# A language-model tower on one core: the first sequence's embedding rules applied by masked matmuls in place of a sort

## The reference

```python
def _L0_tok_ref(token_ids, base_embeddings, rule_transform, token_rules):
    base_embeds = base_embeddings[token_ids]
    rule_indices = token_rules[token_ids]
    rule_matrices = rule_transform[rule_indices]
    return jnp.einsum('bsd,bsde->bse', base_embeds, rule_matrices)

h = _L0_tok_ref(x, base_embeddings, rule_transform, token_rules)
h = h + _L0_attn_ref(_layernorm(h), Q, K, VO)
h = h + _L0_ffn_ref(_layernorm(h), Wg, bg, bias, W1, b1, W2, b2)
```

## Time and profile before

| | us |
|---|---|
| median of 3 runs | 624.54 |
| lowest, highest | 620.55, 628.31 |
| the profiled execution, by its own time | 619.58 |
| its span from first to last instruction | 617.5 |
| PE busy in the span | 499.3 (81%) |
| DVE busy | 410.7 (67%) |
| ACT busy | 287.2 (47%) |
| POOL busy | 228.3 (37%) |

### The profile page before, as it was taken

How to read it: one execution, slowest core, us unless ns; L and a number is a source line. 1 busy time by engine, 2 the same in 40 slices (tenths; PEclk the granted TensorE clock), 3 DMA queues, 4 the chain that set the end, 5 groups by cost and what they waited for, 6 DMA issues and landing times.

```text
span 617.5 us, 9436 instructions
## 1 busy us (share of the span) xinstructions
PE 499.3 (81%) x2732; PEld 268.7 (44%) x2732; DVE 410.7 (67%) x1003; ACT 287.2 (47%) x581; POOL 228.3 (37%) x375
## 2 busy tenths in 40 slices
PE   0066603778679896999999999999999989999985
PEld 0035501234444342445544544454454444575753
DVE  5532486645215874978869877895975776665577
ACT  0203301025545543456564565556456546547664
POOL 5664356463225300340254145122413313181542
PEclk9998755559979997999999999999999999999989
DMA  8815212733381062440440422044042200000000
GB/s 234 312 59 152 79 36 61 179 95 103 95 229 40 14 155 53 102 113 5 100 114 2 102 63 60 1 104 113 1 96 68 53 2 2 11 2 10 11 2 17
DMA packets 21791, 47.05 MB, mean 76 GB/s; under 512 B 6248, under 2 KB 11576, under 8 KB 21680
## 3 DMA queue, kind: packets, MB, share of 16 engines
q1 hardware_dynamic: 15408, 32.23, 21.5%
q0 software_dynamic: 4752, 8.20, 4.9%
q10 hardware_dynamic: 1584, 6.03, 3.0%
HBM read 9.97 MB, written 11.01 MB: 34 GB/s over the span
## 4 chain that ended last, share of the span: by engine, by line
PE 54%; DVE 19%; issue 8%; DMA 6%; POOL 6%; ACT 3%; SPq 3%; another core or an unknown queue 0%; DVEq 0%; ACTq 0%; POOLq 0%
PE bank L1274 14%; PE bank L1260 10%; PE bank L1240 7%; PE bank L1202 4%; PE bank L1224 4%; DVE mx L997 3%; POOL emb_sorted L527 2%; DMA ctxT<-in_table,ids 2%; PE bank L1196 2%; PE bank L1197 2%; DVE r_sb L1055 2%; POOL ctxT L517 2%; PE bank L1132 2%; POOL r_sb L591 2%; DMA ks<-qk_l 1%
## 5 line engine op out<-in xcount | busy, mean ns | idle before, releaser
L997 DVE TENSOR_REDUCE mx<-bank 128x1 f32<-128x512 f32 x256 | 170.5, 687 | 83.5 <-PE bank L1260 75.3
L591 POOL TENSOR_TENSOR r_sb<-r_sb 128x256 f32<-128x256 f32 x174 | 91.0, 523 | 251.8 <-DVE r_sb L1073 171.4
L671 ACT ACTIVATE prob<-bank 128x512 f32<-128x512 f32 x256 | 139.0, 597 | 58.5 <-PE bank L1240 43.0
L1260 PE MATMUL bank<-ks,qs 96*128 96x512 f32 x256 | 122.7, 487 | 14.4 <-DVE mx L997 9.7
L1274 PE MATMUL bank<-prob,xa 128*64 128x512 f32 x448 | 123.5, 630 | 0.7 <-ACT ctxT L685 0.7
L1260 PEld LDWEIGHTS bank<-ks,qs 96*128 96x128 f32 x256 | 50.9, 199 | 130.8 <-issue 109.5
L1240 PE MATMUL bank<-qs,ks 97*128 97x512 f32 x224 | 78.1, 430 | 0.0
L738 ACT ACTIVATE r_sb<-bank,stay 128x512 f32<-128x512 f32 x56 | 37.1, 687 | 44.9 <-PE bank L1197 44.6
L1240 PEld LDWEIGHTS bank<-qs,ks 97*128 97x128 f32 x224 | 38.4, 194 | 15.6 <-issue 11.1
L527 POOL DMA_INDIRECT emb_sorted<-ctxT,pos x32 | 32.0, 1001 | 22.6 <-DMA emb_sorted<-ctxT,pos 11.7
L517 POOL DMA_INDIRECT ctxT<-in_table,ids x32 | 32.4, 1011 | 21.3 <-DMA ctxT<-in_table,ids 8.6
(11 more groups left out here) (167 smaller groups left out, 659.3 us busy)
## 6 DMA issues: line engine op xcount, KB each, us to landing
qs<-qk_h SPq DMA_DIRECT2D x64, 128.0 KB
ks<-qk_h SPq DMA_DIRECT2D x56, 128.0 KB
qs<-qk_l SPq DMA_DIRECT2D x32, 128.0 KB
ks<-qk_l SPq DMA_DIRECT2D x28, 128.0 KB
emb_sorted<-front ACTq DMA_DIRECT2D x4, 608.0 KB
y_sorted<-y_out POOLq DMA_DIRECT2D x19, 128.0 KB, 2.7
e_in<-emb_sorted POOLq DMA_DIRECT2D x9, 256.0 KB, 3.2
emb_sorted<-front ACTq DMA_DIRECT2D x3, 640.0 KB
```

The source lines that it names most:

```text
L591: nc.gpsimd.tensor_tensor(a[:, at:at + width], src[:, 0:width], src[:, width:2 * width], ALU.add).then_inc(S["pool_chain"], 1)
L671: nc.scalar.activation(prob[:, step % NPROB, u % 2, :], bank[u % NST][:], ACT.Exp, scale=SC).then_inc(S["exp_done"], 1)
L997: V.tensor_reduce(mx[:, u // 16, u % 16:u % 16 + 1], bank[3 + n % 2][:], AX.X, ALU.max).then_inc(S["mx_done"], 1)
L1260: M(bank[3 + n % 2][:], qs[0:96, nb % 2, h, tt * 128:(tt + 1) * 128], ks[0:96, nb % 2, h, :], start=True, stop=True).then_inc(S["s_ps"], 1)
```

## The change

Batch 0 is no longer sorted. Its rules are broadcast along a row and its rows are transposed twice (upper and lower 64 partitions). For each of the 50 pairs of rules DVE makes a tile `z`, 128x512, that holds the token's row where its rule is the pair's lower (partitions 0 to 63) or upper rule (64 to 127), and zero elsewhere; PE multiplies it with the pair's two matrices, stacked on 128 partitions of `r_sb`, and accumulates in bank 7, even pairs in its lower and odd pairs in its upper half. The sum is copied and transposed back with both halves added, and DVE copies it to `hbuf`. The matrices are therefore also loaded to partitions 64 to 127, shifted by one rule.

Batch 1 is sorted alone, in tiles of 32 slots (8 groups, 16 small matmuls each), between the masked matmuls; POOL scatters 4 chunks for it where it scattered 8. Batches 2 to 7 keep tiles of 64 slots and 19 groups with another layout of slots, but their `look` for the second and third unit, `starts`, `tile_rules` and `slots` stand later: after batch 0's normalization, and between its row maxima. Their groups stand at steps (0, 6) to (0, 10), four a step. Batch 1's transposes stand at (-1, 15), batch 2's at (1, 0), batch 3's at (1, 6), with the projections behind them. The ten warming matmuls are gone.

```diff
-    WARM = 10
+    NZ = 4
-        R_AT = [(-1, 14), (-1, 15)] + [(0, g // 3) for g in range(18)]
+        R_AT = [(0, 6 + g // 4) for g in range(20)]
-            return {1: (0, 2), 2: (0, 13)}.get(nb, (nb - 2, XT))
+            return {1: (-1, 15), 2: (1, 0), 3: (1, 6)}.get(nb, (nb - 2, XT))
-            return {1: ((0, 2), (0, 2), (0, 3), (0, 3)), 2: ((0, 14), (0, 14), (0, 15), (0, 15))}.get(
+            return {1: ((0, 0), (0, 0), (0, 1), (0, 1)), 2: ((1, 1), (1, 1), (1, 2), (1, 2)), 3: ((1, 8), (1, 9), (1, 10), (1, 11))}.get(
-            N_AT = {1: (0, 0), 2: (0, 10), 3: (0, 14)}
+            N_AT = {1: (-1, 12), 2: (0, 13), 3: (1, 2)}
...
-                if b in (-1, 0):
+                if b in (-1, 0, 1):
                     max_row(b + 1, 0)
                 if 0 <= b + 2 < B:
                     stack(b + 2, 0)
...
-            fetch(range(FIRST + 10))
-            place(0, range(FIRST))
-            bring(0, 0)
+            fetch_four(0, FIRST)
+            fetch(range(FIRST, FIRST + 6))
+            place(0, range(J, FIRST))
+            bring(0, 1)
...
+            act.dma_start(r_sb[D:2 * D, 0:(NR - 1) * D], rules[:, D:NR * D]).then_inc(S["rules_in"], 16)
+            act.dma_start(r_sb[D:2 * D, (NR - 1) * D:NR * D], rules[:, 0:D]).then_inc(S["rules_in"], 16)
...
+                    nc.scalar.copy(y_out[:, (g - 1) % 4, :], bank[2 + (g - 1) % 2][:, 0:4 * D]).then_inc(S["y_ok"], 1)
+            act.wait_ge(S["z_used"], NR // 2)
+            nc.scalar.copy(rb_acc, bank[7][:]).then_inc(S["acc_ok"], 1)
...
-            V.memset(r_sb[D:128, :], 0.0).then_inc(S["rz_ok"], 1)
+            def masked(lo, hi):
+                for i in range(lo, hi):
+                    if i >= NZ:
+                        dve.wait_ge(S["z_used"], i - NZ + 1)
+                    V.scalar_tensor_tensor(z[:, i % NZ, :], rule_row0, pair_id[:, i:i + 1], embT,
+                                           ALU.is_equal, ALU.mult).then_inc(S["z_ok"], 1)
+            masked(0, 3)
             starts(0)
-            slots(0, 0)
+            run(slots(0, 0))
             tile_rules(0)
-            run(look(1, 1))
+            masked(3, 30)
...
+            masked(30, NR // 2)
+            run(look(1, 1))
+            dve.wait_ge(S["h0_ps"], 1)
+            link(V.tensor_copy(hbuf[:, 0:J, :].rearrange("p c d -> p (c d)"), bank[6][:, 0:J * D]))
...
                     run(layernorm(0, "xn_ready"))
+                    run(look(1, 2))
...
                     if (b, k) == (-2, 9):
-                        slots(1, 3)
+                        run(look(1, 3))
+                        starts(1)
                         tile_rules(1)
+                        run(slots(1, 1))
+                        later = chain(slots(1, 2), slots(1, 3))
...
                         V.tensor_reduce(mx[:, u // 16, u % 16:u % 16 + 1], bank[3 + n % 2][:], AX.X, ALU.max).then_inc(S["mx_done"], 1)
+                        if n in (2, 4, 6, 8, 10, 12) or 14 <= n < 20:
+                            next(later, None)
...
-            if k == MT[0] and 0 <= b + 1 < B:
+            if (b, k) == (-1, 11) or k == MT[0] and 0 <= b < B - 1:
                 todo.append(("mt", b + 1, 0))
...
+                ts = TS[int(g >= NG[0])]
+                for q, c, at_ in tile_at[g]:
+                    col = c % 2 * 256 + c // 2 * 128 + q * ts
+                    last = M(out_[q * ts:(q + 1) * ts, c * D:(c + 1) * D], eT[:, g % 2, col:col + ts],
+            for i in range(NR // 2):
+                pe.wait_ge(S["z_ok"], i + 1)
+                half = i % 2 * D
+                M(bank[7][half:half + D, :], r_sb[:, 2 * i * D:(2 * i + 1) * D], z[:, i % NZ, :],
+                  start=i < 2, stop=i >= NR // 2 - 2).then_inc(S["z_used"], 1)
+                if i == 2:
+                    rule_row(0)
+                if i % 4 == 0 and 0 <= i // 4 - 4 <= NG[0]:
+                    group_step(i // 4 - 4)
```

More of the change, by code:

```diff
@@ L821, in slots @@
             def slots(i, q):
-                c0, c1 = q * QC, (q + 1) * QC
-                lo = SPAN[i][0]
-                both, nth, ahead, at_in, past, gap, tile_, hi, mid, low, two = (slot_i[:, j, :] for j in range(11))
-                link(V.tensor_tensor(sel[:], oh[:, c0 - lo:c1 - lo, :], key.unsqueeze(1).to_broadcast([128, QC, NR]), ALU.mult))
-                link(V.tensor_reduce(slot_f[:], sel[:], AX.X, ALU.add))
-                link(V.tensor_tensor(both, slot_f[:], rank[:, c0:c1], ALU.add))
@@ L840, in slots @@
-                link(V.scalar_tensor_tensor(two, two, float(-NG[i] * 512), at_in, ALU.add, ALU.add))
-                V.tensor_tensor(pos[:, c0:c1], two, low, ALU.add).then_inc(S["pos_ok"], 1)
+                c0, c1 = UNITS[q]
+                lo, n = SPAN[i][0], c1 - c0
+                both, nth, ahead, at_in, k, low, dyn, gap, base = (slot_i[:, j, 0:n] for j in range(9))
+                at_, wide, slot_ = home[:, c0:c1], sel[:, 0:n, :], slot_f[:, 0:n]
+                link(V.tensor_tensor(wide, oh[:, c0 - lo:c1 - lo, :], key.unsqueeze(1).to_broadcast([128, n, NR]), ALU.mult))
@@ L870, in _ @@
             V.tensor_scalar(gi[:], ramp_f[:, 0:NE], 1000.0, None, ALU.add).then_inc(S["w_ok"], 1)
-            later = chain(look(1, 2), look(1, 3))
-            for g in range(NG[0]):
-                dve.wait_ge(S["y_ps"], g + 1)
-                store_sent(dve, g - 4)
-                V.tensor_copy(y_out[:, g % 4, :], bank[2 + g % 2][:, 0:4 * D]).then_inc(S["y_ok"], 1)
-                if 5 <= g < 9 or g >= 11:
-                    next(later, None)
-            run(later)
-            starts(1)
-            slots(1, 1)
-            slots(1, 2)
+            masked(30, NR // 2)
+            run(look(1, 1))
+            dve.wait_ge(S["h0_ps"], 1)
+            link(V.tensor_copy(hbuf[:, 0:J, :].rearrange("p c d -> p (c d)"), bank[6][:, 0:J * D]))
             def layernorm(b, done):
```

231 lines of the change are left out of this document (147 added, 84 removed).

## The result

The changed kernel takes 645.74 us, median of 4 runs (644.37 to 649.04), the kernel before 623.14 in 4 runs beside it: ratio 1.041, 95% interval 1.033 to 1.049, **slower by over 2%**. The prediction was 625, between 605 and 645. Ratios and their intervals compare executions in the usual state only; medians take in all, also the few that ran some per cent longer.

The account below looks back on a forecast made before the run. PE was taken to bound from batch 2 on, so step (2, 0) decides: -7 + 3 + 7 = +3 on the profiled 619.6 gives 622.6, set at 625 because the earlier median lay 4.9 above that execution; range 605 to 645.

Parts of the forecast that it names:

- What bounds the kernel: From step (2, 0) on, PE bounds (busy 52.8 of 54.2 us a batch) and that part moves as a block.
- Part 1: Start to batch 0's normalized rows: done at 78 instead of 95.0, 17 us earlier.
- The masked loop: Within Part 1, masked tiles and matmuls: PE is the slower by 9 us, ending at 71 against DVE's 62.
- The 8 us at the low clock: Within Part 1: PE, starting after idling, spends 8 us at the low clock, for 8 matmuls.
- Part 2: Normalized rows to first row maximum, before 16.9: +2 and +3.5 us, so first maximum at 100.4, 11.5 earlier.
- Part 3: First maximum to step (0, 0): the sorted group's wait goes, DVE takes 29.6 us; (0, 0) at 130, 7 earlier.
- Part 4: Steps (0, 0) to (1, 0), before 79.3 us: work moved and new waits sum to +3, bounds -3 and +8.
- Part 5: Steps (1, 0) to (2, 0), before 50.3 us: SP's copies make (1, 7) later; +7, bounds 0 and 10.
- the upper bound's mechanism: In Part 5: the first scores of batch 2, three steps ahead, stop as well, giving 10 us.
- (a): Rival: the tail costs nothing (-1 and 0) and PE keeps near DVE's pace; 606 to 608 us, chance 0.27.
- (b): Rival: PE stays at 1.2 GHz through the masked loop; +25 on the sum, 650 us, chance 0.12.
- (c): Rival: the scatter is late by over 6 us, PE stops at (0, 6); +5 to +12, 633 us, chance 0.13.

Follow-up runs that it names:

- run 1: Changed kernel with ACT waiting for the constants before it issues the second load of the rules: ratio 1.026, 638.6 us against 620.05.
- run 6: Changed kernel with groups at (0, 3) to (0, 7), batches 2 and 3 mostly at old steps, second rules load behind batch 0's gathers: 620.82 us, ratio 1.003.
- Run 2: Kernel before, only with ACT loading the rules a second time, first on its queue, in place of DVE's zeros: ratio 1.011, 627.53 us.
- run 4: Kernel before, with only the places of groups and of batches 2 and 3, and normalization pieces per step, as in the change: ratio 1.042, 648.78 us.
- Runs 3 and 5: Changed kernel, constants first, groups at (0, 3) to (0, 7): 5 so, 1.015, 628.53 us; 3 also batches 2 and 3 mostly at old steps, 1.007, 624.33 us.
- Run 10: The kernel of run 6 with batch 1's normalization, transposes and projections back at (0, 0), (0, 2) and (0, 3): ratio 1.010.

## Why the prediction was wrong, step by step

**What bounds the kernel**: right. From (2, 0) on it moved as a block, by 1.2 us.

**Part 1 is the step that failed most, with 10.9 of the 21.8.** It gave the second load of the rules "between 0 and 3 us, I take 1", as a cost of bandwidth. The load made the constants late by 8.4, at a place that the sum did not look at: the 225.5 KB ahead of the gathers (12.38 for 3.95). What of this reaches masked tile 3, forecast for 31, three fronts show: it came at 38.26 in the changed kernel, at 34.74 in run 1 with the constants first, at 32.49 in run 6 with the load behind the gathers too. So the load cost 5.8 there, 3.5 of it by the constants, and 2.3, inside the 0 to 3, by the gathers. The rest is the sum itself, which had 30 without the load where run 6 has 32.5; there the rows that the first `look` needs came at 20.0 for the 18.1 of before. Run 2 shows the load alone in the old kernel. Run 6 has the normalized rows within 0.3 us of the forecast, but partly by luck: it is 1.5 late at tile 3 and 1.2 quicker behind it. The trace of before had the clue: DVE waited 0.60 for `cst` at 3.95, so the transfer was on the path, and run 2 shows that a load issued at the same time on another queue delays it. The Trainium skill says in "DMA: Bandwidth & Descriptors", section "Queues, rings and completion order", that each DMA engine goes round the queues that have work, packet by packet. The traces agree that the two queues share, with 2.7 and 11.1 us to landing for the same transfer. Why a load of 225.5 KB took as long as one of 1584 KB beside it, no run shows. I had not asked who else was in flight at 1 us.

**The masked loop**, tile 3 to the normalized rows: forecast 47, found 50.6 in the changed kernel, 45.8 in run 6. A mask takes 0.67 (10.69 us for 16 in one row of the changed kernel's DVE), not 0.60: the pricing row was an operation without the pointer to a number per partition. The applies of 32-column tiles take 0.65, not 0.9: 32 records in 0.65 beside 16 of twice the width in 0.69. The Trainium skill's "TensorE: Matmul & The Clock Gate", section "Measured speedup vs the span model", pointed to the lower value; the trace agrees. The 8 us at the low clock did not come: the granted clock was 1.00 from 38 to 82. In run 6 PE and DVE kept nearly the same pace (DVE stood for 1.4 us), where I had PE slower by 9 us. In the changed kernel DVE stood for 6.6, and what was missing in the sum is the pauses: some 5 us, which no run explains.

**Part 2** was right to 0.2 us, and its two terms (look in the shadow of the projections, the rest behind them) with it. **Part 3** had the right mechanism: no wait for a DMA, DVE busy 28.45 of 31.9. Its size was 2.3 short: a maximum by itself takes 0.69 where I had half a pair, 0.65, and small gaps between. POOL's last scatter began 37 us behind the first maximum (148.84) and had landed at 151.29, 39.8 behind it, before the forecast 42.5; no wait for it is left.

**Part 4**, +5.5 for +3. The wait for batch 1's copies was priced at net 2; it took 7.60. The term that failed is the landing, which I had at 2 to 4. From SP's last issue to PE's release, first in the changed kernel, then in run 4:

```profile
154.38 7.68 DMA ks<-qk_l
...
155.92 2.44 DMA ks<-qk_l
```

In the changed kernel POOL issued the first four group loads, of 256 KB each, from 151.29 on, the very moment at which SP began its six copies, and the DMA engines were busy all the time from 154 to 162. In run 4 no group load was in flight. So this looks like part 1 over again: loads whose data PE takes at 171 stand in the way of copies that it needs at once. No run moved these loads alone, so it is read from two traces and not shown by an experiment. At batch 2's rows DVE stopped for 4.61, as forecast (5), but PE stopped for 5.05 where I had counted 3. What the forecast never asked is whether the groups' own place was good. Their data was not late: the four loads landed 3.8 to 8.3 us after their issue, the first by 155, the last by 162, and the first turn, at (0, 6), came at 171.37. Runs 3 and 5 used that slack.

**Part 5**, +11.7 for +7. To (1, 7) it was +6.8 (31.6 for 24.8), as forecast: SP's last issue, the row of maxima, stood at 256.39, 28.1 behind (1, 0), where it had been 19.5. Here the upper bound's mechanism was in it too (first scores of batch 2, 4.83), but inside the same 6.8, not on top. The miss is behind it: from (1, 7) to (2, 0) 30.35 us for 25.45, forecast unchanged. Windows of it, after; the kernel before had 25.10 busy at 0.96:

```profile
259.90:290.25 30.35, 28.74 (x115) 14.43 (x114) 22.02 (x44) 13.57 (x26) 7.24 (x16) 0.87 0.11 24
```

PE was busy for 3.6 us more, with the matmuls of the steps at a lower clock and four of batch 3's projection matmuls more, and stood for 1.3 us more, in one wait of 1.6 for DVE.

**The rivals.** (a), that the tail costs nothing, is refuted: parts 4 and 5 cost 5.5 and 11.7 us where it had -1 and 0, and in run 4 the order alone costs 4.2%. (b), a masked loop at 1.2 GHz, did not happen: the granted clock was 1.00 from 38 to 82, PE 39.0 of 44.0 us busy, though it waited for single tiles. The Trainium skill's "TensorE: Matmul & The Clock Gate", section "Loop structure matters more than you think", had pointed that way, and the trace agrees. (c), a late scatter, did not happen either. The 645 came out by none of them, but by the load at a place that the forecast had not asked about, the unexplained pauses, and its own terms of parts 3 to 5, each too small.

**What the change is worth, taken apart** (ratios to the kernel before; the intervals reach 0.3 to 0.9 points either way and each overlaps the next, so only the way down as a whole is clear): 1.041 as it stands; 1.026 with the constants first; 1.015 with the groups three steps earlier; 1.007 with batches 2 and 3 in their old places; 1.003 with the second load behind the gathers. So the masked multiplication by itself is neither gain nor loss that these runs can tell. It brings batch 0 forward by 16.7 us, and those go back: 5.8 between the normalized rows and the first maximum, where two `look`s and the rest of the second sort now stand; 7.2 before (0, 0), where DVE has 6 us of normalization and two `slots` among the maxima; 3.4 in the first batch's steps, which now hold all groups. Run 10 moved one of these pieces away: 6.0 us less before (0, 0), 10.2 more behind it. No version that I ran beats the kernel before.
